# Attention and feed-forward on one core: weight layout, output buffers and store queues of the head projections

## The reference

```python
q_lat = x @ Wq_down                         # x is already normalised
q_nope = q_lat @ Wq_up;  q_pe = rope(q_lat @ Wq_rope)
kv_lat = x @ Wkv_down
k_nope = kv_lat @ Wk_up; k_pe = rope(x @ Wk_rope);  v = kv_lat @ Wv_up
attn = softmax(where(causal, q @ k.T * 128 ** -0.5, -1e30))
x = x + (attn @ v) @ Wo
# feed-forward on layernorm(x); wu, wg, wd are W_up, W_gate, W_down with
# scale = mean(|W|) + 1e-8 and q = clip(round(W / scale), -1, 1) * scale
x = x + (silu(h @ wu.T) * (h @ wg.T)) @ wd.T
```

## Time and profile before

| | |
|---|---|
| median of 3 runs | 2053.94 us (2053.7 to 2056.29) |
| the profiled execution | 2056.05 us |
| its span, from the first to the last instruction | 2054.3 us |
| mean granted TensorE clock | 0.97 |
| PE busy | 1915.9 us (93%) |
| DVE busy | 1348.4 us (66%) |
| ACT busy | 1053.7 us (51%) |
| POOL busy | 526.1 us (26%) |
| moved by DMA | 157.15 MB |

### The profile page before, as it was taken

How to read it: one execution, slowest core, us unless ns; L and a number is a source line. 1 busy time by engine, 2 the same in 40 slices (tenths; PEclk the granted TensorE clock), 3 DMA queues, 4 the chain that set the end, 5 groups by cost and what they waited for, 6 DMA issues and landing times. The chain is left out here.

```text
span 2054.3 us, 31448 instructions
## 1 busy us (share of the span) xinstructions
PE 1915.9 (93%) x11112; PEld 1658.9 (81%) x11112; DVE 1348.4 (66%) x2833; ACT 1053.7 (51%) x2509; POOL 526.1 (26%) x333
## 2 busy tenths in 40 slices
PE   6988876799999999999999999999999989999999
PEld 4766664699899898899899889979989968787877
DVE  5455554678678788688688778778877863333333
ACT  3233332666566566576576666656756743233232
POOL 6234343523222331331322412322322200000000
PEclk9998988899999999999999999999999999999999
DMA  3598988721120320310302302202212051000000
GB/s 110 144 229 208 228 204 214 220 67 37 54 68 1 89 67 1 89 42 27 89 8 61 89 1 68 67 23 68 47 43 68 1 201 46 20 0 20 0 20 20
DMA packets 66247, 157.15 MB, mean 76 GB/s; under 512 B 7072, under 2 KB 19616, under 8 KB 61984
## 3 DMA queue, kind: packets, MB, share of 16 engines
q1 hardware_dynamic: 66080, 155.09, 27.6%
HBM read 100.53 MB, written 54.53 MB: 75 GB/s over the span
## 5 line engine op out<-in xcount | busy, mean ns | idle before, releaser
L991 ACT CAST turned_hi<-ps_turn 128x512 fp32r<-128x512 f32 (+1 forms) x576 | 314.4, 566 | 387.3 <-PE ps_turn L1159 387.3
L1065 DVE TENSOR_TENSOR turned_lo<-ps_turn,turned_hi 128x512 fp32r<-128x512 f32 (+1 forms) x576 | 370.4, 659 | 129.7 <-ACT turned_hi L991 124.5
L964 ACT ACTIVATE probs<-ps_scores,bias 128x512 f32<-128x512 f32 (+3 forms) x642 | 401.6, 634 | 23.7 <-DVE bias L1058 12.9
L1159 PE MATMUL ps_turn<-ident,probs 128*128 128x128 f32 x2176 | 320.9, 276 | 0.8 <-ACT probs L964 0.2
L1129 PE MATMUL ps_scores<-k_hi,q_hi 128*128 128x512 f32 (+2 forms) x642 | 260.0, 405 | 42.7 <-issue 31.4
L1159 PEld LDWEIGHTS ps_turn<-ident,probs 128*128 128x128 f32 x2176 | 252.0, 141 | 27.1 <-ACT probs L964 3.0
L1032 DVE TENSOR_REDUCE negmax<-ps_scores 128x1 f32<-128x512 f32 x384 | 258.6, 682 | 2.7 <-PE ps_scores L1129 2.4
L1136 PE MATMUL ps_o<-turned_hi,kv_hi 128*128 128x256 f32 x1152 | 247.3, 296 | 4.9 <-DVEq L1064 4.9
L1129 PE MATMUL ps_scores<-k_lo,q_hi 128*128 128x512 f32 (+2 forms) x642 | 239.6, 373 | 0.0
L1129 PE MATMUL ps_scores<-k_hi,q_lo 128*128 128x512 f32 (+2 forms) x642 | 239.3, 373 | 0.0
L1136 PEld LDWEIGHTS ps_o<-turned_hi,kv_hi 128*128 128x128 f32 x1152 | 200.2, 190 | 42.2 <-issue 8.1
(11 more groups left out here) (148 smaller groups left out, 3459.8 us busy)
## 6 DMA issues: line engine op xcount, KB each, us to landing
rotT<-rot_out SPq DMA_DIRECT2D x64, 256.0 KB, 3.6
plainT<-plain_out SPq DMA_DIRECT2D x64, 256.0 KB, 5.1
all_signs<-signs SPq DMA_DIRECT2D x24, 512.0 KB, 5.7
k_raw<-plainT SPq DMA_DIRECT2D x16, 512.0 KB, 5.5
k_raw<-rotT SPq DMA_DIRECT2D x32, 256.0 KB, 6.4
q_raw<-plainT SPq DMA_DIRECT2D x16, 512.0 KB, 8.5
q_raw<-rotT SPq DMA_DIRECT2D x32, 256.0 KB, 8.9
sign_raw<-in_W_up SPq DMA_DIRECT2D x9, 512.0 KB, 7.1
```

What stands on the lines that cost most here:

```text
L964: nc.scalar.activation(probs[:, u % 2, t, first_key:first_key + keys], ps_scores[:, n % RING, 0:keys], ACT.Exp, scale=-1.0 if crosses(u, t ...
L991: nc.scalar.copy(turned_part(0, n, u, s), turned_psum(n, u, s)).then_inc(turned_hi_ready, 1)
L1065: nc.vector.tensor_tensor(turned_part(1, n, u, s), turned_psum(n, u, s), turned_part(0, n, u, s).bitcast(F32), ALU.subtract).then_inc(turn ...
L1159: last = nc.tensor.transpose(ps_turn[:, n % 2, at * P:(at + 1) * P], probs[:, u % 2, t, key:key + P], ident[:])
```

## The change

The host lays out the weights of a pair's nine slices as one array (`by_pair`), already in the order that the rotation wants, so that one DMA loads them and one instruction each makes the high and the low parts. It also lays out, by head, the turned Wv beside Wo (`by_head`); the kernel no longer turns Wv. The combined weights are made for one head at a time, after the plain products of chunks 1 and 3, and of the pair itself. Their high part is copied by ScalarE and their low part made by VectorE at the start of these chunks; one buffer `vo_raw` is loaded again when the low part is done. `rot_out` and `plain_out` have two buffers each for either g, taken by c % 2, each with a semaphore of its own. The plain stores and those of the combined weights are issued by ScalarE, right behind its copy; SP keeps the rot stores and the loads. The split of the following pair's slices moves from chunk 1 to chunk 2.

In `latents`, `AHEAD` goes from 2 to 1, and in each step the latent product comes before the tile that is turned (on TensorE; ScalarE's and VectorE's lists follow that order, VectorE's with the statistics first).

Left out below: ScalarE's and VectorE's reordering in `latents`, declarations of semaphores and their resets at the end of a round.

```diff
 def load_pair_weights(sp, hbm, pair_w, pair, loaded):
-    cols = bass.ds(pair * P, P)
-    for name, s0, k in (("Wq_rope", ROT_Q, KQ), ("Wk_rope", ROT_K, KD), ("Wq_up", PLAIN_Q, KQ), ("Wk_up", PLAIN_K, 1)):
-        sp.dma_start(pair_w["raw"][:, s0:s0 + k, :],
-                     hbm[name].rearrange("(k p) n -> p k n", p=P)[:, :, cols]).then_inc(loaded, 16)
-def pair_views(pair_w, j):
-    raw, (hi, lo) = pair_w["raw"], pair_w["split"][j]
-    views = []
-    for f in range(2):
-        put = [z[:, 0:PLAIN_Q, :].rearrange("p k (f h r) -> p k f h r", h=2, f=2)[:, :, f] for z in (hi, lo)]
-        views.append((raw[:, 0:PLAIN_Q, :].rearrange("p k (h f r) -> p k f h r", h=2, f=2)[:, :, f], *put))
-    views.append(tuple(z[:, PLAIN_Q:NSL, :] for z in (raw, hi, lo)))
-    return views
+    sp.dma_start(pair_w["raw"][:], hbm["pair_w"][bass.ds(pair, 1), :, :].rearrange("a p (k n) -> p (a k) n", n=P)
+                 ).then_inc(loaded, 16)
...
-    AHEAD = 2
+    AHEAD = 1
...
                 for i in range(TC):
+                    if 1 <= c <= NC and i < NL:
+                        latent(c - 1, i)
                     if c < NC:
-                        t = TC * c + i
...
-                        last.then_inc(lat_ready, 1)
+                        turn(TC * c + i)
...
-        wv_raw = sb("wv_raw", [P, 2, P])
-        wvT = [sb(f"wvT_{n}", [P, 2, P], F32R) for n in ("hi", "lo")]
-        wo_raw = sb("wo_raw", [P, 2, D])
-        wo = [sb(f"wo_{n}", [P, 2, D], F32R) for n in ("hi", "lo")]
-        wvo_out = sb("wvo_out", [P, 2, D])
+        vo_raw = sb("vo_raw", [P, P + D])
+        vo = [sb(f"vo_{n}", [P, P + D], F32R) for n in ("hi", "lo")]
+        wvo_out = sb("wvo_out", [P, D])
         ternary_raw = sb("ternary_raw", [P, WCH])
         by_cos = sb("by_cos", [P, 2, CH])
         by_sin = sb("by_sin", [P, 2, CH])
-        rot_out = sb("rot_out", [P, 2, CH])
-        plain_out = sb("plain_out", [P, 2, CH])
+        rot_out = sb("rot_out", [P, 2, 2, CH])
+        plain_out = sb("plain_out", [P, 2, 2, CH])
...
-        def load_weights(sp, pair):
-            heads = bass.ds(pair * 2, 2)
-            load_pair_weights(sp, hbm, pair_w, pair, w_loaded)
-            sp.dma_start(wv_raw[:], hbm["Wv_up"].rearrange("p (h n) -> p h n", n=P)[:, heads, :]
-                         ).then_inc(w_loaded, 16)
-            sp.dma_start(wo_raw[:], hbm["Wo"].rearrange("(h p) n -> p h n", p=P)[:, heads, :]
-                         ).then_inc(w_loaded, 16)
+        VO_AT = (1, 3)
+        def load_vo(sp, head):
+            sp.dma_start(vo_raw[:], hbm["vo_w"][bass.ds(head, 1), :, :]).then_inc(vo_loaded, 16)
...
-            for raw, hi, _lo in pair_views(pair_w, j):
-                last = nc.scalar.copy(hi, raw)
-            last.then_inc(w_hi_ready, 1)
+            nc.scalar.copy(w[j][0][:], pair_w["raw"][:]).then_inc(w_hi_ready, 1)
         def split_lo(j):
-            for raw, hi, lo in pair_views(pair_w, j):
-                last = nc.gpsimd.tensor_tensor(lo, raw, hi.bitcast(F32), ALU.subtract)
-            last.then_inc(w_lo_ready, 1)
+            nc.gpsimd.tensor_tensor(w[j][1][:], pair_w["raw"][:], w[j][0][:].bitcast(F32), ALU.subtract
+                                    ).then_inc(w_lo_ready, 1)
...
+            load_vo(sp, 0)
...
-                    load_weights(sp, following)
+                    load_pair_weights(sp, hbm, pair_w, following, w_loaded)
                     for c in range(NC):
                         toks = slice(c * CH, (c + 1) * CH)
                         for g in range(2):
                             sp.wait_ge(rot_done, PER_PAIR * j + 2 * c + g + 1)
                             sp.dma_start(hbm["rotT"][ROT[g][0], bass.ds(pair, 1), :, toks],
-                                         rot_out[:, g, :]).then_inc(rot_stored[g], 16)
-                        for g in range(2):
-                            sp.wait_ge(plain_done, PER_PAIR * j + 2 * c + g + 1)
-                            sp.dma_start(hbm["plainT"][PLAIN[g][0], bass.ds(pair, 1), :, toks],
-                                         plain_out[:, g, :]).then_inc(plain_stored[g], 16)
+                                         rot_out[:, c % 2, g, :]).then_inc(rot_stored[2 * g + c % 2], 16)
                         if c < len(MATS):
                             sp.wait_ge(abs_done, len(MATS) * j + c + 1)
                             sp.dma_start(ternary_raw[:], hbm[MATS[c]][bass.ds(pair, 1), :, :]
                                          ).then_inc(ternary_loaded, 16)
-                    sp.wait_ge(wvo_copied, j + 1)
-                    sp.dma_start(hbm["wvo"].rearrange("(h p) n -> p h n", p=P)[:, bass.ds(2 * following, 2), :],
-                                 wvo_out[:]).then_inc(wvo_stored, 16)
-                sp.sem_inc(plain_done, -2 * PER_PAIR)
+                        if c in VO_AT:
+                            h = VO_AT.index(c)
+                            head = 2 * pair + h
+                            sp.wait_ge(vo_lo_done, 2 * j + h + 1)
+                            load_vo(sp, (head + 1) % H if h == 0 else 2 * following)
                 sp.sem_inc(rot_done, -2 * PER_PAIR)
-                sp.sem_inc(wvo_copied, -2)
+                sp.sem_inc(vo_lo_done, -4)
                 sp.sem_inc(abs_done, -2 * len(MATS))
+            sp.wait_ge(vo_loaded, 16)
...
-                        if c == NC - 1:
-                            act.wait_ge(wv_turned, j + 1)
-                            nc.scalar.copy(wvT[0][:], ps[:, WV_BANK, 0:2 * P].rearrange("p (h n) -> p h n", h=2)
-                                           ).then_inc(wv_hi_ready, 1)
+                        toks = slice(c * CH, (c + 1) * CH)
+                        if c in VO_AT:
+                            act.wait_ge(vo_loaded, 16)
+                            act.sem_inc(vo_loaded, -16)
+                            nc.scalar.copy(vo[0][:], vo_raw[:]).then_inc(vo_hi_ready, 1)
                         for g in range(2):
                             act.wait_ge(plain_ready, PER_PAIR * j + 2 * c + g + 1)
-                            act.wait_ge(plain_stored[g], 16)
-                            act.sem_inc(plain_stored[g], -16)
-                            nc.scalar.copy(plain_out[:, g, :], ps[:, PLAIN0 + g, :]).then_inc(plain_taken, 1)
+                            act.wait_ge(plain_stored[2 * g + c % 2], 16)
+                            act.sem_inc(plain_stored[2 * g + c % 2], -16)
+                            nc.scalar.copy(plain_out[:, c % 2, g, :], ps[:, PLAIN0 + g, :]).then_inc(plain_taken, 1)
                             act.wait_ge(plain_taken, PER_PAIR * j + 2 * c + g + 1)
                             act.sem_inc(plain_bank_free, 1)
-                            act.sem_inc(plain_done, 1)
+                            act.dma_start(hbm["plainT"][PLAIN[g][0], bass.ds(2 * i + j, 1), :, toks],
+                                          plain_out[:, c % 2, g, :]).then_inc(plain_stored[2 * g + c % 2], 16)
...
-                        if c == 1:
-                            act.wait_ge(w_loaded, 16 * NW * (j + 1))
-                            act.sem_inc(wv_landed, 1)
+                        if c == 2:
+                            act.wait_ge(w_loaded, 16 * (j + 1))
                             split_hi(1 - j)
-                            nc.scalar.copy(wo[0][:], wo_raw[:]).then_inc(wo_hi_ready, 1)
-                    act.wait_ge(wvo_ready, j + 1)
-                    act.wait_ge(wvo_stored, 16)
-                    act.sem_inc(wvo_stored, -16)
-                    nc.scalar.copy(wvo_out[:], ps[:, WVO0:WVO0 + 2, :]).then_inc(wvo_copied, 1)
+                        if c in VO_AT:
+                            h = VO_AT.index(c)
+                            act.wait_ge(wvo_ready, 2 * j + h + 1)
+                            act.wait_ge(wvo_stored, 16)
+                            act.sem_inc(wvo_stored, -16)
+                            nc.scalar.copy(wvo_out[:], ps[:, WVO0, :]).then_inc(wvo_copied, 1)
+                            act.wait_ge(wvo_copied, 2 * j + h + 1)
+                            act.dma_start(hbm["wvo"].rearrange("(h p) n -> h p n", p=P)
+                                          [bass.ds(2 * (2 * i + j) + h, 1), :, :],
+                                          wvo_out[:]).then_inc(wvo_stored, 16)
...
-                            pool.wait_ge(rot_stored[g], 16)
-                            pool.sem_inc(rot_stored[g], -16)
-                            nc.gpsimd.tensor_tensor(rot_out[:, g, :], by_cos[:, g, :], by_sin[:, g, :],
+                            pool.wait_ge(rot_stored[2 * g + c % 2], 16)
+                            pool.sem_inc(rot_stored[2 * g + c % 2], -16)
+                            nc.gpsimd.tensor_tensor(rot_out[:, c % 2, g, :], by_cos[:, g, :], by_sin[:, g, :],
...
-                        if c == 1:
+                        if c == 2:
                             pool.wait_ge(w_hi_ready, j + 1)
                             split_lo(1 - j)
...
```

(51 more changed lines are left out.)

113 lines of the change are left out of this document (54 added, 59 removed).

## The result

| | before | after |
|---|---|---|
| median of 5 runs each | 2053.94 us (2053.7 to 2056.29) | 2042.64 us (2040.51 to 2047.0) |
| the profiled execution | 2056.05 us | 2042.64 us |
| its span | 2054.3 us | 2040.8 us |

The ratio after to before is 0.9946 (95% interval 0.993 to 0.9962): 11.3 us faster, where the forecast was 36. Sign and range held and the size did not.

A forecast was written before the change was run, and what follows sets the result against it. Unlanded stores idle TensorE in the heads; afterwards DMA limits a pair to 30.4 us instead of 35.05. Stage -37, end +3, latents -2 sum to -36: 2020 profiled, 2018 us median, range 1995 to 2045.

The forecast's parts named there:

- The waits name the cause: Head projections: stores not landed keep output buffers and PSUM banks from being free; TensorE idles 38.0 us for plain banks.
- Doubled output buffers: rot_out and plain_out: stores get some 12 us to land instead of 6, worth TensorE's idle 4.75 us a pair.
- Stores issued by ScalarE: Plain and combined-weight stores: 0.45 us an issue on ScalarE, 10 issues or 4.5 us a pair; no bandwidth gained.
- The split chain in chunk 3: ScalarE's, VectorE's and POOL's steps from chunk 2 into chunk 3 delay TensorE's next pair by 2.0 us.
- The late vo load: Load for the next pair's first head, issued after POOL's chunk 3, delays TensorE around chunk 1 by 0 to 1.0 us.
- The DMA floor: A pair's DMA traffic in the heads takes at least 29.2 us at 255 GB/s, 30.4 with a share of 0.96.
- Weights laid out by the host, and no turning of Wv: Heads: fewer loads and copies save 0.4 us of DMA a pair; dropping two Wv transposes is worth at most 0.7.
- The end: End of the heads stage: up to 1 MB more of stores on its way before attention's first load costs 3 us.
- Latents: AHEAD 2 to 1: first latent matmul at about 20.4 instead of 23.11 us; stage gains 2 us.
- The wait only moves: Rival: heads' DMA keeps its gaps at share 0.86, about 1 us a pair gained, 2044 to 2047 us; chance 0.20.
- The split chain decides: Rival: ScalarE, held 10.2 us by stores at chunk 2, delays the low weights; pair 38.4, 2081 us; chance 0.06.

The follow-up runs named there:

- the chain eased: Changed kernel with the following pair's slices split in chunk 1 again on ScalarE and GpSimd: 2019.23 us, 0.9828; with single output buffers too: 2024.77 us, 0.9854.
- Parting VectorE and GpSimd alone: Changed kernel with GpSimd's low part of the slices waiting until VectorE's low part for chunk 3 is done: 2031.02 us, ratio 0.9887.
- the best version: Changed kernel with the split in chunk 1, ScalarE's vo copy ahead of Abs in chunk 2, and the old latents order: 2017.62 us, ratio 0.9816.

## Where the prediction was right, and why it was wrong

The range and the sign were right, the size was three times too large. The step that failed is the sum for a pair, by its term for the new chain in chunk 3: 2.0 us of wait in front of TensorE's next pair, so that TensorE's pair (28.2 to 29.2) lay under the DMA and a pair was 30.4. The rows show 3.5 us of waits and 2.1 us of slow clock behind them in its place. With TensorE's 26.2 these make 31.8 of the 32.6 measured. By the prediction's own steps:

- *"The waits name the cause."* TensorE's 38.0 us did hang on stores that hadn't landed, the first chunk's, and they went. The forecast laid the stall on the weights ahead of these. That is part of it: with the weights behind, the 38.0 became 16.2, and another wait ate the gain (1.0015). What it didn't see is the place behind the rot stores: with the order alone turned the 38.0 became 3.7 and the ratio 0.9912. I read when stores were issued and not when they could have been.
- *"Doubled output buffers": 4.75 us a pair.* Measured: nothing in the kernel after, 5 us of the whole with the chain eased. The 38.0 us go without them too, so the gain can't be booked to the buffers.
- *"Stores issued by ScalarE": the issue's 0.45 us, otherwise nothing.* The issue is 0.34 us. The effect is 32 us on the kernel before and, from 1.007 to 0.9946, some 26 on the changed one. The Trainium skill, DMA: Bandwidth & Descriptors, "Issuing engines are not separate DMA queues", which the forecast weighed, says that a second issuer saves only issue time. From this I took that it gives no bandwidth, and 0.9989 with the ternary loads on it agrees. For this kernel's time the sentence misled me: a second issuer also has a list of its own, without what stands in front in the first.
- *The split chain in chunk 3: 2.0 us a pair.* This is the step that failed. TensorE's waits there are 28.4 us in 8 pairs, 3.5 each, and the slow clock behind them 2.1 in the mean: 5.6 for 2.0. The chain was the forecast's; its terms weren't. VectorE's subtraction was put at 0.8, with GpSimd's low part beside it in the same sum, and took 2.75; ScalarE began Abs late, behind the ternary load, which the sum left out. Parting VectorE and GpSimd alone gives 12 us, parting the whole chain 23.
- *"The late vo load": 0 to 1.0.* No row of after shows TensorE stopped by it in chunk 1, where VectorE's subtraction had 0.83.
- *The DMA floor, 29.2, with a share of 0.96: 30.4.* For the best version it is near: 29.55 at 0.96 and 254 GB/s. The kernel after never got there: its share was 0.84. The share of 0.96 was the wrong choice between 0.86 and 1.01 for this kernel, and 255 GB/s isn't the most that the engines carry (272).
- *Weights laid out by the host, and no turning of Wv.* Not measured by themselves. GpSimd's one instruction took 2.65 us and ScalarE's 1.14, where the forecast took 4.0 and 1.3 as before. The changed kernel is some 20 us slower than the kernel before with ScalarE's stores alone (0.9946 against 0.9841), and the split's move to chunk 2 accounts for it: with the split in chunk 1 the two are level (0.9828). So beside ScalarE's stores the rest of the change gave next to nothing, and the split's move took 23 us back.
- *The end: +3.* Not seen: TensorE's idle time there is 0.7 us shorter. ScalarE's longer wait (13.93 for 9.77) comes of its having finished earlier.
- *Latents: -2.* Measured +2.2. The first product came earlier as forecast (19.85, forecast 20.4), at the lower clock level, and POOL's first start at 20.84 for 21.7. The waits before each later chunk's first product, two of about 0.7 in the forecast, are 2.33, 1.46 and 0.86 (1.73, 0.27 and 0.70 before), and after the longest TensorE is at the lower clock again: 0.52 from 34.6 to 38.0, for 1.00 before. The clock was not in the sum.
- *Rivals.* "The wait only moves" (2044 to 2047) was nearest: share 0.84, though by a new wait on VectorE and not by the single ternary buffer. "The split chain decides" had the right place with a wrong holder: not ScalarE's wait for a store, but GpSimd's hold on VectorE and ScalarE's own order.

## What to carry to other kernels

For each DMA issue ask when its data was ready, and look what stands ahead of it in the same engine's list: a wait for something slower, or the bytes of what isn't urgent, holds every store and load behind it, and two lines exchanged gave here more than doubled buffers. When an edit gives nothing, look whether the wait it aimed at is still there: here it was more than halved, and another had taken its place. Before you put a VectorE subtraction of two SBUF tiles and a GpSimd one into the same chunk, add GpSimd's duration to VectorE's on the path. When one part of a bundle is suspected of carrying it, run that part alone on the old kernel: here it was worth nearly three times the bundle.

## What the runs showed of the hardware

- A VectorE subtraction of 128x640 in SBUF takes 0.83 us alone and up to 2.75 when GpSimd subtracts 128x1152 beside it: in all eight pairs it ended 0.68 us after GpSimd did. With the order forced, 0.82 to 0.83 in all 16.
- After a stop of 1.55 us behind another of 1.77, TensorE's matmuls of 512 columns started 0.45 us apart for seven of them, then 0.23. At the seven pair ends such slow stretches were 7 to 14 matmuls long.
- A DMA issue costs ScalarE's queue 0.34 us.
- In the heads' mix the 16 DMA engines moved 254 GB/s at a share of 0.96 and 272 at 0.99. With the plain stores on ScalarE's queue the kernel before had a share of 0.79 at 247 GB/s, against 0.86 at 216 to 221: the share is no measure of bytes across versions.
